# Layer 3 of a four-layer conditional residual kernel is taken into the transposes ahead of layer 2

## What is computed

```python
x = x + L0(x)   # x @ W0.T + b0, plus a rank-16 LoRA of adapter itok_B_1_7
x = x + L1(x)   # x @ W1.T + b1, plus a rank-16 LoRA of adapter itok_B_6_15
x = x + L2(x)   # x @ weight[itok_B_3_7].T, one of 8 matrices of 1024 x 1024
x = x + L3(x)   # per batch, over the 64 rows: einsum('bct,bcd->bdt', x, W[itok_B_0_15]), W is 64 x 64
```

## Time and profile before

| | us |
|---|---|
| timed runs: 617.97, 620.09, 622.70; median | 620.09 |
| the profiled execution | 617.64 |
| its span, first to last instruction | 615.5 |
| PE busy | 600.7 (98%) |
| weight loads (PEld) busy | 498.7 (81%) |
| DVE, ACT, POOL busy | 304.9, 213.8, 52.8 |
| mean granted clock of PE | 0.996 of 2.4 GHz |

### The profile page before, as it was taken

How to read it: one execution, slowest core, us unless ns; L and a number is a source line. 1 busy time by engine, 2 the same in 40 slices (tenths; PEclk the granted TensorE clock), 3 DMA queues, 4 the chain that set the end, 5 groups by cost and what they waited for, 6 DMA issues and landing times.

```text
span 615.5 us, 10879 instructions
## 1 busy us (share of the span) xinstructions
PE 600.7 (98%) x2838; PEld 498.7 (81%) x2839; DVE 304.9 (50%) x569; ACT 213.8 (35%) x306; POOL 52.8 (9%) x87
## 2 busy tenths in 40 slices
PE   8999999999998999999999999999999979999996
PEld 7888878888887888888888888888888846888885
DVE  6993221032694477454447745344774553543321
ACT  5533211040462365142236524223652343332112
POOL 4350001000120101000002100000210020000000
PEclk9999999999999999999999999999999989999999
DMA  8756723212266325634234563434456363221103
GB/s 302 246 170 67 87 87 140 69 53 69 70 182 214 89 85 174 207 88 117 73 120 114 178 207 88 116 75 120 114 178 206 89 200 90 75 84 35 36 2 70
DMA packets 72156, 73.61 MB, mean 120 GB/s; under 512 B 45122, under 2 KB 53314, under 8 KB 72132
## 3 DMA queue, kind: packets, MB, share of 16 engines
q1 hardware_dynamic: 72132, 73.32, 41.9%
HBM read 62.03 MB, written 11.27 MB: 119 GB/s over the span
## 4 chain that ended last, share of the span: by engine, by line
PE 86%; issue 8%; DMA 2%; DVE 1%; ACT 1%; POOLq 1%; POOL 1%; SPq 0%; ACTq 0%; DVEq 0%
PE y_ps L1045 25%; PE y_ps L1075 24%; PE y_ps L997 11%; PE t_ps L997 5%; PE low_ps L1036 4%; PE t_ps L1104 3%; PE y_ps L978 2%; PE t_ps L1067 2%; DMA arena<-wt 2%; PE y_ps L974 1%; PE low_ps L978 1%; PE t_ps L978 1%; PE y_ps L1059 1%; PE y_ps L1060 1%; PE y_ps L1091 1%
## 5 line engine op out<-in xcount | busy, mean ns | idle before, releaser
L1075 PE MATMUL y_ps<-ring,ops 128*128 128x512 f32 (+1 forms) x792 | 188.2, 394 | 7.3 <-DVE ring L832 5.5
L1045 PE MATMUL y_ps<-wm,ops 128*128 128x512 f32 x768 | 179.8, 390 | 0.0
L1075 PEld LDWEIGHTS y_ps<-ring,ops 128*128 128x128 f32 (+1 forms) x792 | 145.4, 185 | 41.7 <-DVE ring L832 6.4
L1045 PEld LDWEIGHTS y_ps<-wm,ops 128*128 128x128 f32 x768 | 143.0, 188 | 29.2
L997 PE MATMUL y_ps<-ring,wm 128*128 128x512 f32 x240 | 55.3, 390 | 0.0
L832 DVE TENSOR_TENSOR ring<-arena,ring 128x1024 fp32r<-128x1024 f32 x40 | 48.0, 1251 | 12.7 <-ACT ring L529 11.3
L997 PEld LDWEIGHTS y_ps<-ring,wm 128*128 128x128 f32 x240 | 44.9, 188 | 9.3
L848 DVE TENSOR_TENSOR ops<-y_ps,ops 128x1024 fp32r<-128x1024 f32 (+1 forms) x17 | 19.8, 1162 | 62.7 <-ACT ops L547 62.5
L515 ACT CAST side<-a_stage 128x384 fp32r<-128x384 f32 x64 | 28.1, 512 | 61.5 <-DMA a_stage<-a_tab 59.5
L529 ACT CAST ring<-arena 128x1024 fp32r<-128x1024 f32 x40 | 40.4, 1049 | 18.3 <-POOL arena L430 17.8
L436 POOL TENSOR_TENSOR w_stage<-w_stage,ident 128x128 f32<-128x128 f32 x16 | 10.4, 651 | 347.5 <-DMA w_stage<-w 347.5
(11 more groups left out here) (148 smaller groups left out, 585.8 us busy)
## 6 DMA issues: line engine op xcount, KB each, us to landing
arena<-wt SPq DMA_DIRECT2D x48, 512.0 KB, 4.5
arena<-b_tab SPq DMA_DIRECT2D x32, 256.2 KB, 3.3
arena<-xt SPq DMA_DIRECT2D x32, 256.0 KB, 2.8
arena<-b_tab SPq DMA_DIRECT2D x32, 256.0 KB, 3.3
out<-arena SPq DMA_DIRECT2D x30, 256.0 KB, 3.1
arena<-w SPq DMA_DIRECT2D x8, 576.0 KB, 5.3
a_stage<-a_tab SPq DMA_DIRECT2D x64, 64.0 KB, 1.9
arena<-a_cols SPq DMA_DIRECT2D x8, 256.0 KB, 3.7
```

The lines of the kernel that those rows point to most:

```text
L1045: op = nc.tensor.matmul(y_ps[:, cols], xs[:, k, part_x, :], wm[:, k, part_w, cols], start=k == 0 and part_x == part_w, stop=False)
L1075: op = nc.tensor.matmul(y[0:m, cols], xs2[:, k, part_x, 0:m], ring[:, k, part_w, cols], start=k == 0 and part_x == part_w, stop=k == KT - ...
```

## The change

x2 is split before the transposes (`x2_split`: high part on ACT, low part on DVE), and each transpose becomes three products of a block of x2 with the split I + W3: x2's block is the stationary operand, w3 the moving one with 128 columns, so that `t_ps` holds the transposed blocks of layer 3's result. Since layer 3 acts on rows and layer 2 on features, the two may be taken in this order. Layer 2 then gives the final rows, which ACT copies from its result to `out_rows`. The six products of layer 3 and the split of x3 are gone. W3 of pair j is needed a step or two earlier, so its load, fold and split are moved: SP loads w3(j + 1) in step j right behind `load_b` (it waits for the split of w3(j)), ahead of the first chunks and of the store; POOL folds w3(j + 1) in turn j, and w3(0) ahead of the first matrix. `take_out(j - 2)` moves to the head of ACT's step.

```diff
 # SP, step(j)
                     load_b(which)
+                    sp.wait_ge(w3_lo_ready, j + 1)
+                    load_w3(j + 1)
...
                     with sp.If(following != 0):
                         first_chunks(rank + mixed + 2)
-                    sp.wait_ge(w3_lo_ready, j - 1)
-                    load_w3(j - 1)
                     store(j - 2)
 # POOL
+            fold_w3(0)
             fold(0)
             pool.wait_ge(plan_ready, 1)
-            with pool.Fori(0, PAIRS) as j:
-                pool.wait_ge(w3_in, 32 * j + 32)
-                nc.gpsimd.tensor_tensor(w3_stage[:, :], w3_stage[:, :], ident[:, :], ALU.add).then_inc(w3_folded, 1)
+            with pool.Fori(0, PAIRS - 1) as j:
+                fold_w3(j + 1)
                 rank, mixed, following = first_rank(pool, j), mixed_of(pool, j), following_of(pool, j)
 # ACT
+            def x2_hi(j):
+                act.wait_ge(x2_ready, j + 1)
+                if not (isinstance(j, int) and j == 0):
+                    act.wait_ge(t_done, j)
+                nc.scalar.copy(x2_split[:, 0, :], x2).then_inc(x2_hi_ready, 1)
...
+            def take_out(j, y=y2_ps, banks=(slice(0, FEATS),)):
+                act.wait_ge(stored, 32 * j + 16)
                 for n, cols in enumerate(banks):
                     act.wait_ge(l2_done, j + (1 + n))
-                    nc.scalar.copy(x3[:, 0, cols], y[:, cols]).then_inc(x3_hi_ready, 1)
+                    nc.scalar.copy(out_rows[:, cols], y[:, cols]).then_inc(out_ready, 1)
...
                 if before == 2:
-                    x3_hi(j - 2)
+                    take_out(j - 2)
                     xs2_hi(j - 1, 1)
-                    split_w3(j - 2)
                     second_half_of_next(j - 2)
...
                 if not last:
                     a_hi(j + 1)
-                if before == 2:
-                    take_out(j - 2)
...
+                split_w3(j)
                 if not last:
                     x_hi(j + 1, 0)
...
                     x_hi(j + 1, 1)
+                x2_hi(j)
+                if not last:
                     b_hi_parts(j + 1)
 # DVE
+            def x2_lo(j):
+                dve.wait_ge(x2_hi_ready, j + 1)
+                nc.vector.tensor_tensor(x2_split[:, 1, :], x2, x2_split[:, 0, :], ALU.subtract).then_inc(x2_lo_ready, 1)
...
-                if before == 2:
-                    x3_lo(j - 2)
                 low(j, 0)
...
                     xs2_lo(j - 1, 1)
-                    split_w3(j - 2)
                     second_half_of_next(j - 2)
...
                     a_lo(j + 1)
...
+                split_w3(j)
                 if not last:
                     x_lo(j + 1, 0)
...
                 take_x2(j)
+                x2_lo(j)
                 if not last:
                     b_lo_parts(j + 1)
 # PE
             def transposes(j):
-                pe.wait_ge(x2_ready, j + 1)
+
+                pe.wait_ge(x2_lo_ready, j + 1)
+                pe.wait_ge(w3_lo_ready, j + 1)
+                if not (isinstance(j, int) and j == 0):
+                    pe.wait_ge(xs2_lo_ready, 2 * j)
                 for k in range(KT):
                     cols = slice(k * P, (k + 1) * P)
-                    op = nc.tensor.transpose(t_ps[:, cols], x2[:, cols], ident[:, :])
+                    for part_x, part_w in SPLIT:
+                        op = nc.tensor.matmul(t_ps[:, cols], x2_split[:, part_x, cols], w3_split[:, part_w, :],
+                                              start=part_x == part_w, stop=part_x == 1)
                 op.then_inc(t_done, 1)
...
-            def layer3(j, last=False):
...
                     elif not (isinstance(i, int) and i == 0):
-                        pe.wait_ge(x3_lo_ready, i)
+                        pe.wait_ge(out_ready, i)
...
-                if before == 2:
-                    layer3(j - 2)
...
-            layer2(PAIRS - 1, lambda: layer3(PAIRS - 2), y=y_ps, last=True)
-            layer3(PAIRS - 1, last=True)
+            layer2(PAIRS - 1, lambda: None, y=y_ps, last=True)
```

More of the change, by code:

```diff
@@ L106, in build @@
         at += 2 * FEATS
-        x3 = ops[:, at:at + 2 * FEATS].rearrange("p (s n) -> p s n", s=2)
-        acc_w_split = x3
+        x2_split = ops[:, at:at + 2 * FEATS].rearrange("p (s n) -> p s n", s=2)
+        acc_w_split = x2_split
         at += 2 * FEATS
@@ L441, in _ @@
                     fold(rank + mixed + 1)
+            rank, mixed = first_rank(pool, PAIRS - 1), mixed_of(pool, PAIRS - 1)
+            with pool.If(mixed != 0):
+                fold(rank + 1)
         def x_of(h):
@@ L541, in xs2_hi, with split_w3 @@
                 nc.scalar.copy(xs2_of(h, 0), t_of(h)).then_inc(xs2_hi_ready, 1)
-            def x3_hi(j, y=y2_ps, banks=(slice(0, FEATS),)):
-                act.wait_ge(l3_done, j + 1)
+            def x2_hi(j):
[3 more added lines that the diff above has]
+                nc.scalar.copy(x2_split[:, 0, :], x2).then_inc(x2_hi_ready, 1)
+            def split_w3(j):
+                act.wait_ge(w3_folded, j + 1)
+                if not (isinstance(j, int) and j == 0):
+                    act.wait_ge(t_done, j)
+                nc.scalar.copy(w3_split[:, 0, :], w3_stage[:, :]).then_inc(w3_hi_ready, 1)
+            def take_out(j, y=y2_ps, banks=(slice(0, FEATS),)):
+                act.wait_ge(stored, 32 * j + 16)
                 for n, cols in enumerate(banks):
                     act.wait_ge(l2_done, j + (1 + n))
-                    nc.scalar.copy(x3[:, 0, cols], y[:, cols]).then_inc(x3_hi_ready, 1)
[L549 to L558, removed]
+                    nc.scalar.copy(out_rows[:, cols], y[:, cols]).then_inc(out_ready, 1)
             def second_half_of_next(j):
@@ L630, in _ @@
                 convert_mixed(rank, j - 1)
[L631 to L633 removed]
+            take_out(j - 1, y_ps, BANKS)
         @block.vector
@@ L843, in xs2_lo @@
                 nc.vector.tensor_tensor(xs2_of(h, 1), t_of(h), xs2_of(h, 0), ALU.subtract).then_inc(xs2_lo_ready, 1)
[L845 to L848, removed]
+            def x2_lo(j):
+                dve.wait_ge(x2_hi_ready, j + 1)
+                nc.vector.tensor_tensor(x2_split[:, 1, :], x2, x2_split[:, 0, :], ALU.subtract).then_inc(x2_lo_ready, 1)
             def split_w3(j):
                 dve.wait_ge(w3_hi_ready, j + 1)
-                nc.vector.tensor_tensor(w3_lo[:, :], w3_stage[:, :], w3_hi[:, :], ALU.subtract).then_inc(w3_lo_ready, 1)
+                nc.vector.tensor_tensor(w3_split[:, 1, :], w3_stage[:, :], w3_split[:, 0, :], ALU.subtract).then_inc(w3_lo_ready, 1)
             def second_half_of_next(j):
@@ L1093, in layer2_by_banks @@
                     op.then_inc(l2_done, 1)
-            def layer3(j, last=False):
-                pe.wait_ge(w3_lo_ready, j + 1)
-                if not last:
-                    pe.wait_ge(xs2_lo_ready, 2 * j + 4)
-                else:
-                    pe.wait_ge(out_ready, PAIRS - 1)
-                for n, cols in enumerate(BANKS):
-                    pe.wait_ge(x3_lo_ready, j + 1 + (n if last else 0))
-                    for w, part in ((w3_hi, 0), (w3_lo, 0), (w3_hi, 1)):
-                        op = nc.tensor.matmul(t_ps[:, cols], w[:, :], x3[:, part, cols],
-                                              start=w is w3_hi and part == 0, stop=part == 1)
-                    if last or n == NB - 1:
-                        op.then_inc(l3_done, 1)
             def layer2(i, between, y=y2_ps, last=False):
@@ L1158, in step @@
                     pe.wait_ge(xs2_lo_ready, 2)
-                def next_transposes():
-                    if before == 2:
-                        pe.wait_ge(out_ready, j - 1)
-                    transposes(j)
                 if before >= 1:
-                    layer2(j - 1, next_transposes)
-            pe.sem_inc(l3_done, 1)
+                    layer2(j - 1, lambda: transposes(j))
             pe.wait_ge(ident_ready, 1)
```

23 lines of the change are left out of this document (8 added, 15 removed).

## The result

The changed kernel takes 631.32 us in the median of four runs (629.52 to 632.79) against 620.00 of the kernel before on the same chip (617.97 to 622.70): ratio 1.0193, 95% interval 1.0161 to 1.0225. The forecast was 627.3, with a range of 616 to 635. The profiled execution took 632.79 us, its span is 630.6 (before 615.5). Direction and range held, but the sum on which the forecast stands was +7.3 us and the two spans are 15.1 apart.

What follows compares the result with a forecast made beforehand. PE, busy 98% of the span, was taken as the bound. Terms 3.8 + 6.5 - 0.7 - 1.38 - 2.36 + 0.6 + 0.8 = +7.3 us gave 624.9 profiled, 627.3 on the timed runs' scale; range 616 to 635.

Steps and rivals of the forecast that it cites:

- The crux: Price on PE of one product of 128 columns, set by its weight load: 0.115 us, ends 0.108 and 0.120.
- the block's +1.89: 24 products in the transposes' place take 2.76 us against 0.87, so +1.89 us a block.
- The exchange of block and layer 3: In a steady step the block adds 1.89 us and layer 3 leaves (-1.38): net +0.50 us.
- The split of x2: Late only in steps 4, 8 and 12, 0.2 us each: 0.6 us in all, ends 0 and 1.5.
- What goes behind the loop (-3.74): Behind the loop, layer 3 of pair 14 goes (-1.38 us) and the tail before the final copy goes (-2.36).
- Step 12: Mixed pair's step: two PE waits become one of about 4 us, slow clock likely: -0.7 us, ends -6 and +0.5.
- Rivals 1 to 5: Hidden loads 609.7 us (0.08); 81 ns products 615 (0.05); split late 642 (0.08); loads unoverlapped 653 (0.03); step 12 without wait 622 (0.16).
- in step 1 that cover is missing: In step 1 x2's low part delays DVE, so PE waits about 1.1 us: +0.8 us, ends 0 and 2.
- Queues. ... Cost nothing: SP's new wait for the split of w3 costs nothing; if the cover fails, 0 to 2 us once.
- the wait for chunk 7 hid those 1.4 to 1.5 us; afterwards nothing would: In step 12 the slow clock after PE's idle time, hidden before, would lengthen the last half by 1.4 to 1.5 us.

Runs made afterwards that it cites:

- Experiments 2 and 3: Changed kernel with each of the 24 products made as two of 64 moving columns (e_m64), or with 64 stationary columns (e_s64): 703.03 and 616.74 us.
- experiment 5: Changed kernel with 48 already fulfilled waits ahead of step 0 in PE's stream, moving later code: 626.95 us, ratio 1.0137.
- e_mix: Changed kernel with e_hoist's early register loads and the mixed pair's chunks converted and issued earlier: 617.54 us, ratio 0.9984.
- the two shifts of the kernel before: Kernel before with 24 or 48 fulfilled waits ahead of step 0 in PE's stream: 619.08 and 617.92 us, one execution each.
- e_hoist: Changed kernel with PE's two register loads for layer 2 ahead of the second half of the main product: 626.54 us, ratio 1.0131.
- e_mixpad: e_mix with 48 fulfilled waits ahead of step 0 in PE's stream: 617.58 us, ratio 0.9977.
- b_mix: Kernel before with the mixed pair's chunks earlier and POOL folding them ahead of w3: 610.60 us, ratio 0.9869.
- e_s64: Changed kernel with stationary operands of 64 columns in place of 128, half the features left out: 616.74 us, ratio 0.9944.
- e_m64: Changed kernel with each of the 24 products made as two of 64 moving columns: 703.03 us, ratio 1.1351.

## Why the prediction was right in direction, and 8 us short

**Right.** The crux, a product of 128 columns, was read off one product in the trace of before as 0.115 us, bound by its weight load; it is 0.110 (2.63/24), so that the block's +1.89 was +1.76, with 0.08 more on the half behind it. Experiments 2 and 3 show that the load is what binds. By the Trainium skill, TensorE: Matmul & The Clock Gate, the section Back-to-back issue gap has 81 ns for this product, and the rule of the section LDWEIGHTS, columns over 1.2 GHz, gives 107 ns for its load as an estimate; the traces agree with the second (110 measured) and not with the first. The exchange of block and layer 3 came to 0.48 us a step for 0.50. The split of x2 was never late (0 for 0.6, within its ends of 0 and 1.5). What goes behind the loop (-3.74) is exact: the final copy starts with the last product's end, which answers to the earlier trace rows:

```profile
626.57 0.59 ACT L563 COPY arena<-y_ps 128x512 f32<-128x512 f32 x1 [2.08 <-PE y_ps L1090]
```

Step 12 went from two waits to one, whose end was put at 37.5 us from the step's start and came at 37.6 (525.17 less 487.57). Rivals 1 to 5 are all refuted by the block's 2.63 us, by steps of 27.49, and by the 4.43 us of step 12.

**Wrong, first: "The split of x2 ... in step 1 that cover is missing ... I put +0.8; ends 0 and 2".** The wait itself was even shorter than I said (0.64 us for 1.1), and with the two blocks it comes to about the 4.5 us of experiment 5. That this sum fits is partly luck. Up to layer 2, step 1 goes by DVE and not by PE's products: DVE's split of `t_ps` ended 2.50 us later than before (188.66 for 186.16), because DVE's last piece of low(1, 0) ended 2.0 us later (179.68 for 177.69) and two conversions behind that took 2.87 us for 2.35; PE's own products had moved by 2.76 us, nearly the same. The other part of the 4.5 is the second block. But the step cost 10.0, because PE's sequencer stood 3.7 us at a branch, and the clock fell: it was 0.63 in the window from 193.90, behind 4.92 us of idle time. The step that failed is the bound: I took DVE's margin for all that could be late in step 1. I had named PE's wait for DVE ahead of the first layer 2, but not what its row in PE's timeline of before holds beside that wait:

```profile
188.22 5.75 PE L1075 MATMUL y_ps<-ring,ops 128*128 128x512 f32 x24 [1.81 <-issue]
```

DVE's split ends at 186.16 and layer 2 starts at 188.22: the register loads and the branch lie on the path between them, so whatever lengthens them counts in full. Experiment 5 shows that moving the code takes the long branch away, 5.5 us of step 1. That it is a fetch of code is not shown by an edit of its own, but argued from the transfers on the instruction queue, whose end lies 1.37 to 1.38 us ahead of the branch's end in all three traces that have a long branch; the Trainium skill, Runtime: NRT & Kernel Launch, section Instruction fetch mechanics, says that a taken branch whose target isn't in the two pages at hand has to wait until its page is fetched; the traces agree, with a transfer of 16 KB in the midst of each long branch. Against a simple rule stand e_mix, with the long branch in the profiled run and, by its times, not in eight of ten, and the two shifts of the kernel before, which brought none about.

**Wrong, second: "Queues. ... Cost nothing".** I went through SP's and POOL's queues and the waits of ACT and DVE, and not through PE's own sequencer. Layer 3 was cover: its 1.38 us on PE were slack for `low(j, 1)` on DVE and for the register loads behind it, in the steps in which four conversions stand ahead of it. I named that wait for step 1 only. Taken away, it cost 3 x 0.83 = 2.5 us, and e_hoist gives all of it back.

**Wrong, third, a size: "the wait for chunk 7 hid those 1.4 to 1.5 us; afterwards nothing would".** The mechanism was right, a slow clock in the last half. The half took 8.02 us, 2.3 over the 5.7 of a full clock, 0.9 more than the 7.14 that I took from the earlier trace rows. Step 12 was +0.1 for -0.7.

**What the change is worth without these.** Compare e_mixpad with b_mix, which share the earlier chunks and have neither long branch nor slow last half: spans of 615.5 and 609.0, medians of 617.58 and 610.60, so 6.5 and 7.0 us. The blocks cost more than layer 3 and the tail give back, by nearly what the sum of +7.3 said. e_mixpad also has the register loads ahead, which b_mix hasn't, and which save the idle time ahead of layer 2 in step 1 (1.69 us in experiment 5); by these numbers the two would be some 8 us apart without them, an estimate.

Open: what decides from one execution to the next whether the branch is long.

## What to carry to other kernels

- In this kernel a product costs its weight load when it has no more moving columns than stationary ones: 0.110 us for 128 stationary columns, whether 128 or 64 columns move. Folding a small product into transposes makes three such loads out of each transpose, and pays only where the product that it replaces costs more than twice the transposes' time.
- Work that goes from the bottleneck engine takes its cover along. List for each step what waits in parallel behind it, the engine's own sequencer (register loads, branches) included, and do it for the steps in which another queue is loaded, not for the average one.
- An "issue" gap in the profile of before can mark a place where the sequencer is already on the path, behind a wait that the profile doesn't name: compare its end with the ends on the other engines. Load registers where a long run of products covers them.

## What the runs showed of the hardware that I had not expected

PE's granted clock can fall while PE has no idle time, in and behind stretches of narrow products. In e_m64 PE does not wait once between 200 and 690 us, and yet the clock falls to 0.50 again and again, as in the windows above; all its steps there are longer than the 30.1 us that the products alone would make. In e_hoist it happens once, in step 1, right behind the first of the step's two blocks, some 3 us behind a wait of 0.64 us. PE's timeline comes first, then the windows:

```profile
179.74 0.33 PE L1045 MATMUL low_ps<-low_split,g_split 128*128 128x128 f32 x1 [0.64 <-DVE low_split L827]
179.90 3.01 PE L1065 MATMUL t_ps<-w_split,ops 128*128 128x128 f32 x24
182.71 7.16 PE L1038 MATMUL y_ps<-wm,ops 128*128 128x512 f32 x24
```

```profile
180.50:182.70 2.20, 2.20 (x21) 2.20 (x20) 2.18 (x4) 0.54 (x2) 2.04 (x2) 0.94 0.56 166
182.80:184.50 1.70, 1.70 (x5) 1.34 (x5) 1.39 (x5) 1.70 (x4) 0.00 (x0) 0.50 0.70 191
```

The 24 products of L1038 behind it take 7.16 us in place of some 5.7. In the changed kernel the same products, behind the same block and the same wait, kept the full clock (1.00 from 182 to 186 us), so the block alone doesn't decide it. A fall costs 1.5 to 2.4 us: 7.16 here, and 8.07 and 8.02 in the changed kernel behind 4.92 and 4.43 us of idle time, against 5.6 to 5.7 at the full clock. PE's branch into layer 2 of step 1, which took 0.23 to 0.48 us in the other nine profiled executions, took 3.73, 3.85 and 5.83 us in three (the changed kernel, e_s64, e_mix).
